# Another order of the 1003 steps of a two-layer macaron block, written out by hand as a string

## The reference

```
x = x + 0.5 * int_ffn(norm(x))      # quantise rows to int8, times int8 weight, scales, bias
x = x + attention0(norm(x))         # 16 heads of width 8, rope, causal softmax, W_O
x = x + 0.5 * int_ffn(norm(x))
x = x + 0.5 * gated_ffn(norm(x))    # silu(x Wg) * (x Wu), times Wd; hidden width 384
x = x + attention1(norm(x))         # 16 heads of width 64, causal softmax, w_o
x = x + 0.5 * gated_ffn(norm(x))
```

## Time and profile before

| | |
|---|---|
| median of 3 runs | 772.33 us (766.01 to 773.03) |
| the profiled execution's own time | 767.38 us |
| its span | 765.6 us |
| mean granted clock of TensorE | 0.964 of full |
| TensorE busy | 703.4 us, 92% |
| VectorE busy | 531.1 us, 69% |
| GpSimd busy | 487.9 us, 64% |
| ScalarE busy | 432.5 us, 56% |

### The profile page before, as it was taken

The page is one execution under the profiler, slowest core; times in us unless marked ns, Lnnn a source line. Parts: engine busy times, 40 slices in busy tenths (PEclk is TensorE's granted clock), DMA queues, the critical chain, the costliest instruction groups (busy, mean ns, idle before and its releaser), DMA issues.

```text
span 765.6 us, 21561 instructions
## 1 busy us (share of the span) xinstructions
PE 703.4 (92%) x9385; PEld 422.7 (55%) x9387; DVE 531.1 (69%) x731; ACT 432.5 (56%) x530; POOL 487.9 (64%) x387
## 2 busy tenths in 40 slices
PE   2668988898889899999999999999999999999997
PEld 1534445445435364666555665655786555666854
DVE  7598889989988876786866666766246786452137
ACT  2334676987778678545556654553607556555312
POOL 6823456306863400499999899975629996989740
PEclk9855899999999999999999999999999999999999
DMA  8000000000000000001001101100101101112000
GB/s 281 2 2 2 3 2 3 3 3 3 3 2 3 2 3 2 3 2 31 22 10 29 30 4 30 30 30 3 30 2 30 31 3 30 30 30 58 30 1 28
DMA packets 13225, 16.20 MB, mean 21 GB/s; under 512 B 3052, under 2 KB 10572, under 8 KB 13132
## 3 DMA queue, kind: packets, MB, share of 16 engines
q1 hardware_dynamic: 12556, 14.50, 6.6%
q10 hardware_dynamic: 576, 0.33, 0.1%
HBM read 13.26 MB, written 1.17 MB: 19 GB/s over the span
## 4 chain that ended last, share of the span: by engine, by line
PE 67%; DVE 12%; POOL 10%; ACT 7%; issue 3%; DMA 0%; POOLq 0%; ACTq 0%; DVEq 0%
PE ps L1291 18%; PE ps L1240 15%; DVE big L1103 9%; PE ps L1210 5%; PE ps L1457 5%; ACT Pr L714 5%; PE ps L1270 4%; POOL acts L696 3%; PE ps L1464 3%; POOL V0s L696 2%; PE ps L1406 2%; PE ps L1301 2%; PE ps L1496 2%; PE ps L1414 1%; PE ps L1426 1%
## 5 line engine op out<-in xcount | busy, mean ns | idle before, releaser
L714 ACT ACTIVATE Pr<-ps 128x1024 f32<-128x1024 f32 (+1 forms) x272 | 251.1, 977 | 126.0 <-PE ps L1291 42.6
L696 POOL TENSOR_TENSOR V0s<-V0s,Pr 128x1024 f32<-128x1024 f32 x77 | 181.3, 2354 | 102.0 <-PE ps L1240 78.1
L1134 DVE TENSOR_REDUCE mxb<-ps 128x8 f32<-128x1024 f32 (+1 forms) x147 | 172.3, 1197 | 80.2 <-PE ps L1291 55.1
L1103 DVE TENSOR_REDUCE big<-ps 128x8 f32<-128x1024 f32 (+1 forms) x168 | 171.0, 1065 | 17.4 <-PE ps L1270 11.7
L1291 PE MATMUL ps<-big 64*128 64x128 f16 (+2 forms) x2560 | 167.5, 259 | 0.2 <-ACT Pr L714 0.2
L1270 PE MATMUL ps<-big 32*128 32x128 f16 (+2 forms) x1280 | 102.1, 278 | 28.7 <-DVE big L1103 15.0
L1291 PEld LDWEIGHTS ps<-big 64*128 64x128 f16 x2560 | 92.9, 94 | 62.7 <-issue 17.3
L1240 PE MATMUL ps<-Pr,V1s 128*64 128x128 f32 (+2 forms) x960 | 105.5, 368 | 0.0
L1270 PEld LDWEIGHTS ps<-big 32*128 32x128 f16 x1280 | 43.1, 95 | 102.3 <-ACT Pr L714 39.2
L696 POOL TENSOR_TENSOR acts<-acts,Pr 128x1024 f32<-128x1024 f32 x35 | 82.5, 2356 | 12.3 <-PE ps L1240 7.9
L1210 PE MATMUL ps<-Pr,V0s 128*18 128x128 f32 (+2 forms) x1280 | 81.4, 379 | 0.2 <-ACT Pr L721 0.2
(11 more groups left out here) (245 smaller groups left out, 910.6 us busy)
## 6 DMA issues: line engine op xcount, KB each, us to landing
rec_b<-scratch_dram SPq DMA_DIRECT2D x30, 256.0 KB, 3.9
X<-in_x_dram SPq DMA_DIRECT2D x2, 256.0 KB, 3.6
big<-in_pick_rows_dram SPq DMA_DIRECT2D x2, 256.0 KB, 3.0
X<-in_x_dram SPq DMA_DIRECT2D x1, 512.0 KB, 5.6
rec_b<-in_w_q_dram SPq DMA_DIRECT2D x1, 512.0 KB, 6.0
XT<-in_w_k_dram SPq DMA_DIRECT2D x1, 512.0 KB, 6.8
XT<-in_w_v_dram SPq DMA_DIRECT2D x1, 512.0 KB, 7.6
wo_s<-in_w_o_dram SPq DMA_DIRECT2D x1, 512.0 KB, 8.5
```

Source lines behind the costliest of these rows:

```text
L696: g.tensor_tensor(dst, dst, src, ALU.add).then_inc(summed, 1)
L714: ins = a.activation(dst[:, part], src, func, scale=scale)
L1103: ins = v.tensor_reduce(maxima_of(mall[:, r, 2 * u:2 * u + 2][:, part], i), block_view(src, i), AX.X, ALU.max, negate=True)
L1134: ins = v.tensor_reduce(maxima_of(mxb[:, r][:, part], arg), block_view(src, arg), AX.X, ALU.max, negate=True)
```

## The change

The string ORDER is written anew in ten of its eleven lines. Every letter occurs as often as before, so the steps, their instructions and the waits in the code are the same and only their order, the banks that follow from it and the values waited for differ. The first 34 letters stay. The rest of the kernel is untouched.

```diff
--- before.py
+++ after.py
@@ -187,16 +187,16 @@
 
 
 ORDER = (
-    "ammmmmmmmmammmmmmmmmmmtammheeemehwmemwhememmehewemewmemwmmwehmememehmemwtheahwmeehwemewemegemewmemwe"
-    "memwmehhmewmmhmememmehwememwmhmthmwmhmhhmememwmehewemgeemhmwhemhwmeehwmeamewememtemwemememwmemwemwem"
-    "amewemewemewememewemewemmeewhmmwtmemwhmegememwemegmahhmmwmheheweehmwmemwemhmheewemewemetmehmemwmemwm"
-    "emhahwememhehewemewemewmememwemwemhemheetwemhhhhhwhhhwhhwhemhemgmehemwemheewhemwememememwemwemwemewm"
-    "mhemwmKQQtVVMegeeMweMeweMeweMeweMeweMeweMeweeMgeewTKKQwwMMgEEEMWMMWWMMVhMEEMEEEEMMWWMMKQhTWWWWhMEhSM"
-    "EhEhMWWMhEEMEEMEMWTEMMWWWWMMEWWhMEVhKQWWMEEMhEEMMWWWWTSMhEEEEhMWMMKVQWWMEEEEMWMMMWWWMESTMEMWMEEEMKhQ"
-    "WWMhhhWWEMEEEMTShhhWWWMhEEEEEVhhhWWWMMMhWhWWMEEEMWWMEEMhQKVSTMhhEEEMWWWWWWMEMWMEMWMEEEhWWMMQKWSTEMEE"
-    "EEMWMMQKVWMMMWWWMEEMEEMMWWMMSTWMEEEEEQVKMMWWWWWWMEEMEEMTSMEEMWWMMMWWWWWMEEEMWWMEEEEEEESTVKOOQOOMMMWW"
-    "WWhWWMEEMQKVVMMWWhWMEEMEEEEMSTMEMWWMMMWWWWMEEKhQWWWMEEMEEMhhhhWWWMEETSMEMWhMMMWWWMEEMVhhQVKhhhWWSTME"
-    "EEEWMMWWMEEEEEMWWWWWWEMhMWWMMKhQVVSTMEEEEEEEEMWWWWMMMWWWEMMWWMEEMhSTEEEEEEWWWWWWWEEEEEESEEWWOOOOWWWW"
+    "ammmmmmmmmammmmmmmmmmmtammheeemehwhmemwheememmehwemewmemwmmwemememehmemwthheawmeehwemewemegemewmemwe"
+    "mhemwmemwmmhmemhemmehwmewmemetmwmmhhhmhhmememwmheewemgeehmmwehmhwmeehwmeamewememtemwemememwmemwemwem"
+    "amewemewemewememewemewemmeewhmmwtmemwhmegememwemegmahhmmwmheeweehmwmemwemhmehhewemewemetmememwmemwme"
+    "mhhahwemwemhehehwemewememememwemwememhetewemhhhhhwhhhwhhwhemhemgmehemwemheewemwememememwemwemwemewhm"
+    "mhwemmKQQtVVMegeeMweMeweMeweMeweMeweMeweMeweeMgeewTKKQwwMMgEEEMWMEEMWWMMVhMEEMEEMMWWMMKQhTWWWWhMEhSh"
+    "MEhEMWWMhEEMEEMEEMWWWTMMWWWMMEWhMEVhQKWWMEEMEhEMMWWWWTSMhEEEEhMWMMQKVWWMEEEEMWMMMWWWMESTMEMWMEEMKhQW"
+    "WMEhhhhWWEMEEEMSThhWWWMhEEEEEhVhhWWWMMMhWWhWMEEMWWWMEEMhQKVSTMhhEEEEMWWWWMEMWWMEEMWMEhWWMMKQSTWMEEEE"
+    "EEMWMMQKVWMMMWWWMEEMEEEMMWWWMMSTWMEEEEQVKMMWWWWWMEEMEEMTSMEEMWWMMMWWWWWMEEEMWWMEEEEEEESTVKOOOQOMMMWW"
+    "WWWhWWMEEMQKVVMMWWMhEEMEEMSTMEMWWMMMWWWMEEEEKhQWWWWMEEMEEMEhhhhWWWMTSMhEMWMMMWWWMEEEMVhhQVKhhhWWSTME"
+    "EWEMMWWMEEEEEEMWWWWWWEMhMWWMMKQVVSTMEEEEEEEEMWWhWWMMMWWWEMMWWMEEMhSTEEEEEEWWWWWWWEEEEESEEEWWOOOOWWWW"
     "WWW"
 )
 LEFT = {letter: iter(steps) for letter, steps in streams().items()}
```

## The result

The changed kernel takes **774.77 us** (median of 17 runs, 770.64 to 783.98) against 770.33 us for the kernel before in 17 runs of the same session (765.24 to 773.17). The ratio is 1.006, 95% interval 1.0039 to 1.008: slower by 0.6%, some 4.6 us. The forecast was 768.5 us, 1.4 us faster. Its range holds the time and its view of the kernel before (769.9 us in the middle) was right, but the sign was not.

A forecast was written before the change was run, and what follows sets the result against it. VectorE and TensorE were taken to set the pace in the first attention, TensorE from 305 to 737 us. Terms 0 + 0.3 - 0.6 - 1.2 + 0 + 0.1 + 0 = -1.4 took 769.9 to 768.5 us, range 758 to 777.

The forecast's parts named there:

- (b): Turned norm and query-key product of batch 1, 109 to 129 us: -0.5 for a saved wait, +0.8 for a hole, +0.3 us.
- (d): Pair 4's first exponentials, 402 to 410 us: TensorE's 1.28 us gap goes as their scores move behind five steps, -1.2 us.
- (e): Other gaps of the TensorE-bound half stay; a late GpSimd addition is covered and other swaps are harmless: 0, at most +1 us.
- (a): Peak of the quantised norm, 73 to 78 us: GpSimd's second half could start 0.9 us sooner, but counted 0, bounds +-1.0 us.
- slower rival: ScalarE, waiting for the late rope, keeps exponentials back and the clock falls twice more, 118 to 150 us: 776 us, chance 0.15.
- (c): Group 5's three weighings, 217 to 226 us, go up one to three TensorE steps and avoid a clock drop: -0.6 us.
- (f): Banks dealt anew: steps evicted in two instructions go from 45 to 47, +0.1 us, at most +0.3.
- (g): The end, around GpSimd's seven additions from 716.44 us: earlier TensorE savings come through, 0 of its own.
- the drops differ between runs: Clock drops fall where a thin stretch happens to lie, not by the order: 769.1 us, chance 0.2.

The follow-up runs named there:

- r1_first: Kernel before with only the moves among the first 100 letters (until about 107 us): median 768.71 us, ratio 0.9988.
- r2_rope: Kernel before with only the moves of letters 101 to 200 (about 107 to 142 us): median 771.66 us, ratio 1.0015.
- r9_pk: Kernel before with only the scores of pair 4's first exponentials moved behind other steps: median 769.01 us, ratio 1.0001.
- r5_qk: Kernel before with only letters 102 to 120 moved, xt and qk of batch 1 behind more maxima and exponentials: median 771.76 us, ratio 1.0012.
- r6_v: Kernel before with only letters 121 to 136 moved, v of batch 1 two maxima later, the turn and two weighings earlier: median 771.95 us, ratio 1.0011.
- third part: Kernel before with only the moves of letters 201 to 420 (about 170 to 285 us), norms of batch 0 and group 5's weighings: median 772.92 us, ratio 1.0013.
- r8_split: Kernel before with only the last split of batch 0's last gated layer moved 17 letters back: median 770.16 us, ratio 1.0003.
- r4_pairs: Kernel before with only the moves from letter 421 on, nearly all in the second attention: median 771.76 us, ratio 1.0012.
- k2_after: Changed kernel with 22 added products, results overwritten, before first maxima to keep TensorE active: median 775.08 us, ratio 1.0064 against the kernel before.
- k1_before: Kernel before with 22 added products, results overwritten, before first maxima to keep TensorE active: median 768.52 us, ratio 1.0001.
- k3_first: Kernel before with the moves among the first 100 letters and 22 added products that keep TensorE active: median 769.87 us, ratio 0.9998.

## Why the prediction was wrong

The sum was -1.4 us; measured are +3.0 us at equal clock and +1.2 us by the clock. The step that failed is (b), which took over VectorE's gapless stretch from the old profile (+0.3 forecast, +1.6 measured); (d) and (e) failed too, by 1.0 and 0.7 us. That the time lies within the range is owed to the range's width. By its own steps:

**(a) right.** GpSimd's second half of the norm starts at 76.79 instead of 78.55 us, 1.0 us sooner against the start of the order, as forecast 0.9, and it is worth nothing (r1_first, -0.1 +- 0.5). That VectorE's and TensorE's queues cover it fits this number; by itself it wasn't tried.

**(b) wrong, the costliest step.** Forecast +0.3, measured +1.6 +- 0.5 (r2_rope). The rope starts 2.4 us later against VectorE (forecast 2.3), the gap of 0.49 us goes, and the first hole nets +0.2 to +0.3 as summed. But that sum came out by luck: the gain ahead of the hole is 1.4 us, not 0.5, and the hole is 1.54 us, not 0.8, since an exponential's scores stand between qk and the next maximum's. Wrong was the sentence that VectorE "runs on from 122.08 us for 12.16 us without a gap", taken over from the old profile although the same change moves v past two maxima toward the second qk. That puts two products of 2 us nearly side by side and opens a hole of 1.22 us. I had followed ScalarE's queue behind the rope and not asked what stood between the long TensorE steps. ScalarE's wait, forecast near 4 us, is 0.15: the exponentials that moved back to it filled the time. The changed kernel, ScalarE:

```profile
124.72 1.15 ACT L818 ACTIVATE big<-V1s 128x512 f16<-128x512 f32 x2 [0.15 <-POOL V1s L664]
```

So the slower rival had the place but not the mechanism: ScalarE's lateness didn't decide, VectorE's lack of scores did.

**(c) the sign at its place came true, the gain not, and the mechanism isn't shown.** The clock stays up from 219.6 to 223 us, and group 5's first weighing takes 1.07 us as forecast, at 218.90 us. But r9_pk, r5_qk and r6_v, where this weighing stands in its old place, are at full clock from 219.6 to 223 us too, so nothing shows that the weighing did it. (It goes up by four TensorE steps and the other two by three, not by one to three.) And the clock falls elsewhere instead. Changed kernel, sums by short stretch:

```profile
173.20:176.40 3.20, 3.20 (x48) 1.53 (x44) 2.00 (x5) 1.97 (x3) 1.13 (x1) 0.50 0.03 5
207.30:214.00 6.70, 6.70 (x91) 3.41 (x88) 4.29 (x4) 2.36 (x4) 5.35 (x3) 0.50 0.01 4
...
219.60:223.00 3.40, 2.82 (x36) 0.75 (x26) 3.27 (x9) 2.74 (x4) 2.12 (x1) 1.00 0.01 2
227.80:231.10 3.30, 3.11 (x38) 1.36 (x38) 2.37 (x4) 1.41 (x2) 2.90 (x6) 0.50 0.02 5
```

The drops at 76.2, 219.6 and 260.5 us are traded for ones at 173, 207 (twice as long), 228 and 753 us. Forecast -0.6, measured for the third part +0.3 +- 0.5 at equal clock and +1.4 by a clock whose interval includes 0.

**(d) wrong.** Forecast -1.2, measured -0.2 +- 0.5 (r9_pk). The step moves behind seven others, not five. Half of the gap moved to the next step, which I hadn't looked at, and the rest was given back at a sum that waits for GpSimd. I had called GpSimd second in this half and then reckoned as if TensorE alone set its time. Its busy time from 305 to 545 us is 238.1 us as before, where 239 was to show the gain.

**(e) wrong in one move.** I counted the splits' moves at 0 since TensorE is busy throughout; the last split, behind seven additions on GpSimd's queue, costs +0.7 (r8_split). The long move on GpSimd that I did price, the norm before an addition, is not seen in r4_pairs: r8_split's piece alone accounts for all of its 0.7 us, each to 0.5 us.

**(f), (g)** can't be told apart from 0 by these runs.

The parts add: -0.1 + 1.6 + 0.3 + 0.7 = 2.5 against 3.0 +- 0.5, each of them +- 0.5. The clock's share (+1.2) is less settled. The changed kernel has 4.3 +- 3.1 us more at half speed than the kernel before, and k2_after 7.1 +- 6.5 us more than k1_before, so in both pairs the new order has more of it. But no single part shows it clearly, and the kernel before itself averaged from 60.4 to 65.7 us in its four sets of runs.

That the drops differ between runs was right as a rival. Whether they have a tie to the order can't be told from one profile of each kernel, though they fall in a pattern. Six profiles (the kernel before, r1_first, r4_pairs, r8_split, k1_before, k3_first) have their last two drops before 300 us at 217 to 220 and at 258 to 261 us. r9_pk has the same letters until 400 us, and its drops are at 206.7 and 261.4. All five with the third part's new letters have drops at 207 to 210 and at 228 to 231 us. But the three with its old letters and a changed rope stretch (r2_rope, r5_qk, r6_v) have them at 210 to 213 and at 224 to 227 us, so it isn't the third part's letters alone that move them. What does wasn't tried.

## What to carry to other kernels

When steps are put in another order, write out each engine's own queue and, in it, what the pace-setting engine gets between any two long steps of its supplier. A gapless stretch in the old profile is no cover for a change that moves the steps that made it gapless. In a half where TensorE is busy throughout, look for the sums and splits that wait for the second engine; a gap closed ahead of such a sum was given back (r9_pk), and a split slid behind seven additions cost what it made TensorE wait, 0.6 to 0.7 us (r8_split). And where one kernel's runs spread by the clock, fit the time to the granted clock first: here it made intervals of 2 us into ones of 0.5.

## What the runs showed of the hardware

A microsecond at half speed costs 0.276 +- 0.012 us on average over the runs, about a quarter, where it would be half if all of the kernel's time were TensorE's. From 39 to 61 us, where VectorE sets the pace at a granted clock of 0.50, its maxima run without a gap from one to the next; 11.6 us less at half speed, bought with 22 products more, were worth 1.2 +- 1.5 us net. The same program shows 0.949 to 0.971 of full clock from run to run, and with it 774.2 to 764.7 us.
